# Dynamic filters: squares of two tile pairs summed on TensorE instead of GpSimd, and TensorE's sums placed between the next chunk's taps

## The reference

```python
h = x
for _ in range(5):
    t = gelu(einsum('oc,bchw->bohw', W1, h) + b1)
    k = einsum('oc,bchw->bohw', W2, t) + b2          # C * 9 channels
    k = k.reshape(B, C, 9, H, W)
    k = k / (norm(k, axis=2) + EPS)
    y = sum(patches(h) * k, axis=2)                  # 3x3 neighbourhood
    h = h + alpha * y
```

## Time and profile before

| | |
|---|---|
| median of 3 runs | 20082.18 us (20081.55 to 20100.58) |
| the profiled execution's own time | 20080.48 us |
| its span | 20078.7 us |
| layer of dynamic filters in it | about 15,565 to 20,079 us |
| TensorE matmul / VectorE / ScalarE / GpSimd busy over the whole span | 62% / 52% / 28% / 47% |
| mean granted TensorE clock over the whole span | 0.736 |

### The profile page before, as it was taken

The page is one execution under the profiler, slowest core; times in us unless marked ns, Lnnn a source line. Parts: engine busy times, 40 slices in busy tenths (PEclk is TensorE's granted clock), DMA queues, the critical chain, the costliest instruction groups (busy, mean ns, idle before and its releaser), DMA issues. The chain is left out here.

```text
span 20078.7 us, 217701 instructions
## 1 busy us (share of the span) xinstructions
PE 12353.6 (62%) x73490; PEld 6114.7 (30%) x73490; DVE 10535.6 (52%) x14652; ACT 5526.4 (28%) x7765; POOL 9453.1 (47%) x8026
## 2 busy tenths in 40 slices
PE   5553699999999202333333333333358899999998
PEld 2551366666666101111111111111112333333332
DVE  4557544444444333443443444344422788888887
ACT  1114333333333000000000000000010666666666
POOL 0113100000000106886887788688800787878787
PEclk9999856656666556666666666666679999999999
DMA  4104222222222494335334433533342112121201
GB/s 94 33 21 102 55 38 36 37 38 36 36 37 38 135 195 111 95 95 131 95 95 107 120 95 95 131 96 95 95 86 58 33 22 42 21 42 22 42 19 30
DMA packets 1399772, 1408.47 MB, mean 70 GB/s; under 512 B 771709, under 2 KB 1116045, under 8 KB 1383565
## 3 DMA queue, kind: packets, MB, share of 16 engines
q1 hardware_dynamic: 1106892, 742.84, 18.5%
q0 software_dynamic: 221184, 604.27, 10.4%
q10 hardware_dynamic: 70976, 50.83, 0.8%
HBM read 1036.74 MB, written 276.84 MB: 65 GB/s over the span
## 5 line engine op out<-in xcount | busy, mean ns | idle before, releaser
L1359 POOL DMA_INDIRECT dc_g<-corners,dc_idx x4608 | 5253.7, 1140 | 1326.0 <-issue 1260.9
L1954 POOL TENSOR_TENSOR df_sq<-df_sq 128x512 f32<-128x512 f32 x1920 | 2713.0, 1427 | 1866.6 <-ACT df_sq L1902 1839.5
L1432 PE MATMUL dc_ps<-ident,dc_s 128*128 128x128 f32 x2560 | 674.0, 428 | 4296.9 <-DVE dc_s L1523 4294.8
L1079 POOL TENSOR_TENSOR nz_vp<-nz_vp,nz_den 128x2048 f32<-128x2048 f32 x16 | 105.8, 6610 | 4814.7 <-DMA nz_den<-den_d 4814.7
L1515 DVE TENSOR_TENSOR dc_g<-dc_g,dc_wt 128x2304 f32<-128x2304 f32 x512 | 1308.6, 2556 | 2001.0 <-DMA dc_g<-corners,dc_idx 2000.9
L1902 ACT ACTIVATE df_sq<-df_pk,vecs 128x512 f32<-128x512 f32 x2880 | 1921.1, 685 | 1326.0 <-DVE df_pr L2056 1309.2
L2056 DVE SCALAR_TENSOR_TENSOR df_pr<-df_pk,vecs,df_h 128x512 f32<-128x512 f32 x2880 | 2047.6, 741 | 407.1 <-PE df_pk L1840 264.5
L1432 PEld LDWEIGHTS dc_ps<-ident,dc_s 128*128 128x128 f32 x2560 | 472.0, 218 | 4480.6 <-DVE dc_s L1523 3352.1
L1392 ACT ACTIVATE dc_st<-dc_ps 128x512 f32<-128x512 f32 x640 | 327.0, 607 | 4934.2 <-PE dc_ps L1432 4934.2
L1840 PE MATMUL df_pk<-df_t,df_wp 64*128 64x512 f32 x3840 | 1389.8, 642 | 364.7 <-ACT df_sq L1902 302.1
L916 DVE TENSOR_REDUCE at_mx<-at_pt 128x4 f32<-128x512 f32 x1024 | 707.8, 691 | 1605.4 <-PE at_pt L779 1605.4
(11 more groups left out here) (271 smaller groups left out, 19428.1 us busy)
## 6 DMA issues: line engine op xcount, KB each, us to landing
df_h<-df_h SPq DMA_DIRECT2D x160, 512.0 KB, 7.1
dc_g<-corners,dc_idx POOLq DMA_INDIRECT x4608, 2.8
corners<-dc_xt SPq DMA_DIRECT2D x16, 4160.0 KB, 41.5
dc_xp<-x SPq DMA_DIRECT2D x8, 4096.0 KB, 40.8
cv_xp<-x SPq DMA_DIRECT2D x8, 4096.0 KB, 50.0
y<-sp_p SPq DMA_DIRECT2D x128, 192.0 KB, 2.8
y<-sp_p SPq DMA_DIRECT2D x64, 384.0 KB, 4.3
at_a<-y SPq DMA_DIRECT2D x64, 384.0 KB
```

Source lines behind the costliest of these rows:

```text
L1359: nc.gpsimd.indirect_dma_start(gt[:, r, k, :, :].rearrange("p a c -> p (a c)"), None, image, bass.IndirectOffsetOnAxis(ap=idx[:, s, r, k:k ...
L1432: i = nc.tensor.transpose(ps[:, j, 128 * r:128 * r + 128], sm[:, r % 2, 128 * j:128 * j + 128], env.ident[:, :])
L1954: nc.gpsimd.tensor_tensor(a, a, sq[:, (KK * n + other) % RING, :], ALU.add).then_inc(nadded, 1)
```

## The change

GpSimd adds squares 2 into 0 and 3 into 1, as before, and no longer 4 into 0 and 5 into 1: four adds a chunk are left (`ADDS = 4`). TensorE sums the tiles 0 and 1 and the tiles 4 and 5 of the squares, four matmuls in place of two. `sums` is split into `products(n, i)` with i = 0 to 3 and `squares(n, i)` with i = 0 and 1, two matmuls each. They are set between the taps of the next chunk. The joins of VectorE are split: the squares of chunk n - 1 are joined behind product 7 and the products of chunk n - 2 behind product 1. The rings hold 18 tiles. ScalarE's `root`, `log` and `seed` stand one tap later, and so do VectorE's checks and most of its refinements.

```diff
-    BANKS, RING = 5, 15
+    BANKS, RING = 5, 18
+    ADDS = 4
...
-            def sums(n):
-                pe.wait_ge(product, KK * n + KK)
-                if n:
+            def products(n, i):
+                pe.wait_ge(product, KK * n + (2 * i + 2 if i < 3 else KK))
+                if i == 0 and n:
                     pe.wait_ge(yjoined, n)
...
+                for s in range(2):
+                    half = py[64 * s:64 * s + 64, :]
+                    if i < 3:
+                        last = nc.tensor.matmul(half, pair[:, :], pr[:, (KK * n + 2 * i + s) % RING, :], start=(i == 0), stop=False,
+                                                tile_position=(0, 64 * s))
+                    else:
+                        last = nc.tensor.matmul(half, env.ident[:, 64 * s:64 * s + 64], pr[:, (KK * n + 8) % RING, :],
+                                                start=False, stop=True, tile_position=(0, 64 * s))
                 last.then_inc(ysummed, 1)
...
+            def squares(n, i):
+                if i == 0:
+                    pe.wait_ge(nadded, ADDS * n + 2)
+                    if n:
+                        pe.wait_ge(njoined, n)
+                else:
+                    pe.wait_ge(squared, KK * n + 6)
+                for s in range(2):
+                    k = 4 * i + s
+                    last = nc.tensor.matmul(pn[64 * s:64 * s + 64, :], pair[:, :], sq[:, (KK * n + k) % RING, :],
+                                            start=(i == 0), stop=(i == 1), tile_position=(0, 64 * s))
+                if i == 1:
+                    last.then_inc(nsummed, 1)
...
             for n in range(NC):
-                for k in range(6):
-                    tap(n, k)
-                if n:
-                    sums(n - 1)
+                for i in range(3):
+                    tap(n, 2 * i)
+                    tap(n, 2 * i + 1)
+                    if n:
+                        products(n - 1, 0) if i == 2 else squares(n - 1, i)
                 if n + 1 < NC:
                     hid(n + 1)
                 for k in range(6, KK):
                     tap(n, k)
-            sums(NC - 1)
+                    if n:
+                        products(n - 1, k - 5)
...
# ScalarE
-                if k == 6 and n:
-                    act.wait_ge(nsummed, n)
...
-                    if q and (c, k) in ((0, 7), (0, 8)):
-                        root(q - 1, k - 7)
-                    if q and (c, k) in ((1, 0), (1, 1)):
-                        log(q - 1, k)
-                    if q and (c, k) in ((1, 2), (1, 3)):
-                        seed(q - 1, k - 2)
+                    if q and (c, k) in ((0, 8), (1, 0)):
+                        root(q - 1, c)
+                    if q and (c, k) in ((1, 1), (1, 2)):
+                        log(q - 1, k - 1)
+                    if q and (c, k) in ((1, 3), (1, 4)):
+                        seed(q - 1, k - 3)
...
# GpSimd
-                add(n, 0, 4, 1)
-                add(n, 1, 5, 2)
+                singles(n)
                 if q and c == 2:
                     scale(q - 1, 2)
-                singles(n)
                 add(n, 6, 7)
...
# VectorE
-            CHECK = {(1, 6): 0, (1, 8): 1, (2, 1): 2, (2, 3): 3}
-            REFINE = {(2, 5): 0, (2, 7): 1, (3, 1): 2, (3, 3): 3}
+            CHECK = {(1, 7): 0, (2, 0): 1, (2, 2): 2, (2, 4): 3}
+            REFINE = {(2, 6): 0, (2, 8): 1, (3, 2): 2, (3, 4): 3}
...
+                    if n >= 2 and k in (0, 2, 4, 8):
+                        dve.wait_ge(ysummed, 4 * (n - 2) + min(k // 2, 3) + 1)
+                    if n >= 2 and k == 6:
+                        dve.wait_ge(yjoined, n - 1)
...
-                    if k == 5 and n:
-                        join(n - 1)
+                    if k == 1 and n >= 2:
+                        join_products(n - 2)
+                    if k == 7 and n:
+                        join_squares(n - 1)
```

More of the change, by code:

```diff
@@ L1843, in tap @@
                     nc.tensor.matmul(pk[:, j % BANKS, :], ws[:, k - 6, :], t[:, n % 2, :], start=True, stop=True).then_inc(tapped, 1)
-            def sums(n):
-                pe.wait_ge(product, KK * n + KK)
-                if n:
+            def products(n, i):
+                pe.wait_ge(product, KK * n + (2 * i + 2 if i < 3 else KK))
+                if i == 0 and n:
                     pe.wait_ge(yjoined, n)
-                for k in range(6):
-                    s = k % 2
-                    nc.tensor.matmul(py[64 * s:64 * s + 64, :], pair[:, :], pr[:, (KK * n + k) % RING, :], start=(k < 2), stop=False,
-                                     tile_position=(0, 64 * s))
@@ L1853, in sums @@
                 for s in range(2):
-                    last = nc.tensor.matmul(py[64 * s:64 * s + 64, :], env.ident[:, 64 * s:64 * s + 64],
-                                            pr[:, (KK * n + 8) % RING, :], start=False, stop=True, tile_position=(0, 64 * s))
-                last.then_inc(ysummed, 1)
-                pe.wait_ge(nadded, 6 * n + 4)
-                if n:
-                    pe.wait_ge(njoined, n)
-                for s in range(2):
-                    last = nc.tensor.matmul(pn[64 * s:64 * s + 64, :], pair[:, :], sq[:, (KK * n + s) % RING, :], start=True, stop=True,
-                                            tile_position=(0, 64 * s))
@@ L1863, in sums @@
-                last.then_inc(nsummed, 1)
+                    half = py[64 * s:64 * s + 64, :]
[5 more added lines that the diff above has]
+                                                start=False, stop=True, tile_position=(0, 64 * s))
@@ L1875, in _ @@
                     tap(n, k)
-            sums(NC - 1)
+                    if n:
+                        products(n - 1, k - 5)
+            for i in range(2):
+                squares(NC - 1, i)
+            for i in range(4):
+                products(NC - 1, i)
         @block.scalar
@@ L1951, in add @@
                 if earlier:
-                    pool.wait_ge(nadded, 6 * n + earlier)
+                    pool.wait_ge(nadded, ADDS * n + earlier)
                 a = sq[:, (KK * n + into) % RING, :]
@@ L1980, in _ @@
                     scale(q - 1, 3)
-                add(n, 6, 8, 5)
+                add(n, 6, 8, 3)
                 if q and c == 1:
@@ L1992, in _, with join_products, join_squares @@
             dve.wait_ge(link, 3)
-            def join(n):
+            def join_products(n):
                 q, c = n // CH, n % CH
-                dve.wait_ge(ysummed, n + 1)
+                dve.wait_ge(ysummed, 4 * n + 4)
                 dve.wait_ge(sadded, n + 1)
                 nc.vector.tensor_tensor(yr[:, q % 2, c, :], py[:, :], pr[:, (KK * n + 6) % RING, :], ALU.add).then_inc(yjoined, 1)
+            def join_squares(n):
+                q, c = n // CH, n % CH
                 dve.wait_ge(nsummed, n + 1)
-                dve.wait_ge(nadded, 6 * n + 6)
+                dve.wait_ge(nadded, ADDS * n + ADDS)
                 nc.vector.tensor_tensor(nr[:, q % 2, c, :], pn[:, :], sq[:, (KK * n + 6) % RING, :], ALU.add).then_inc(njoined, 1)
@@ L2068, in _ @@
                         refine(q - 1, REFINE[c, k])
-            join(NC - 1)
+            join_products(NC - 2)
+            join_squares(NC - 1)
+            join_products(NC - 1)
             for i in range(CH):
```

## The result

The changed kernel takes 20266.86 us (median of 4, 20258.59 to 20272.56) against 20081.86 us before (median of 4). The ratio is 1.009, with a 95% interval from 1.0073 to 1.0108: 185 us slower. The profiled execution took 20262.01 us, its span is 20260.1 us.

The account below looks back on a forecast made before the run. TensorE was taken to bound three of four chunks, ScalarE c = 1. From 20082 us, three 13.15 us chunks less 1.11 in c = 1 add 79, clock falls 68: 20229, forecast 20230 us, 8-in-10 range 19985 to 20325.

Parts of the forecast that it names:

- the sign: Whole kernel: chances against the time before were slower 0.70, faster 0.17, the same 0.13.
- Changes of split: TensorE's order: 12 changes a chunk at 0.14 or 0.20 us, 2.0 us, making the chunk 13.15 us.
- The two kinds that had no row: Whole array to sums, sums to half-row taps: unseen before, together 0 to 1.02 us a chunk; upper end taken.
- Bank waits: TensorE's taps waiting for squares to free a bank: the new order leaves at least 5 us, so these waits go.
- Chunk c = 1: ScalarE's chunk: 16.28 us instead of 17.39, a gain of 1.11 us, with TensorE idle 3.1 us at its end.
- the moved square: ScalarE's stretch in c = 1: one of seven squares goes ahead of it, worth 0.57 us, leaving 15.58 us.
- The clock: TensorE after idling in c = 1: a fall costs up to 1.7 us; one in two groups assumed, +68 us.
- VectorE: Work unchanged, c = 2 about 13.3 us, level with TensorE; join done by about 5.6 us, products at 6: no wait, but closely.
- GpSimd, nothing on the path: GpSimd's dropped adds: 913 us of busy time go, but 0 on the path.
- The rivals: Three other outcomes for the whole kernel: faster (0.17), no change (0.13), slower still (0.08), against forecast 0.62.
- The faster one: Unseen changes of split on TensorE cost little: chunk 12.47 us, kernel 19998 us; with nothing 12.13 and 19919; chance 0.17.
- slower still: VectorE's join late in c = 0 and c = 2, product 8 late in c = 0: +160 us, 20390 us; chance 0.08.

Follow-up runs that it names:

- e3: Changed kernel's work in another TensorE order, five changes of split a chunk in place of 12, sums in longer blocks: 19904.04 us, ratio 0.9906.
- e6: Changed kernel with ScalarE's root, log and seed put back one tap earlier, where the kernel before has them: 20053.78 us, ratio 0.9985.
- e2: The order alone: changed kernel with all six adds on GpSimd and one pair of squares on TensorE: 20188.68 us, ratio 1.0048.
- e7: e3 with ScalarE's root, log and seed one tap earlier: 19951.98 us, ratio 0.9933.
- e4: Changed kernel plus three unused whole-array matmuls on TensorE at the end of each chunk c = 1: 20166.28 us, ratio 1.0037.
- e5: e3 with the old division of work, six adds on GpSimd and one pair of squares on TensorE: 19961.14 us, ratio 0.9937.

## Why the prediction was right, and where it was off

The time lies in the range, 37 us above the forecast of 20230 us, and the sign was given 0.70.

- **Changes of split.** Right, and shown: 1.01 to 1.06 us for each step that follows another kind. The two kinds that had no row came in at the upper bound. A chunk is 13.27 us, not 13.15: with 2.0 us for twelve changes I had rounded each down by about 0.01 us. Over three chunks and 80 groups that is 29 us too little. (In the rival's sum the low end of 12.13 us a chunk gives 19916 us, not 19919.) e3 shows the reverse: seven changes fewer, 1.2 us a chunk.
- **Bank waits.** Right: TensorE waits for no square in c = 2, 3 and 0, where all the time is busy.
- **Chunk c = 1.** Right in size, 16.28 us, and 2.95 us of idle time where 3.1 was worked out. The sum holds, but the sentence that counts the moved square as a gain of 0.57 us hides that the move itself costs 1.5 us (e6), since the stretch also starts 2.07 us later, the distance from tap 7 to tap 8.
- **The clock.** Right in kind, small in size: 1.6 us a fall, but in 52 of 64 groups instead of in half. That is 0.45 us a group more, 36 us.
- **VectorE.** This step was off, in the harmless direction. I had its work unchanged and c = 2 at about 13.3 us, level with TensorE; it is 10.37 us there, mostly since checks and refinements became shorter. And I had the first products 6 us after tap 0 and the join done by 5.6. My own prices put these products at 5.2 us (three pairs of taps, two of squares, each with a change of split), which with a join at 5.6 is a miss of 0.4 us. The trace has 5.19 and 4.59. That the meeting is met was right by luck.
- **GpSimd, nothing on the path.** This step was off for the same reason: I left out that its adds lengthen VectorE's operations. With six adds the join would come too late even for the changed kernel's place (e2, worked out and not run by itself). And in the groups with `residual`, where VectorE does come late in c = 0, the price fell. These are 14 and not 16, as the last two of the 16 do this work behind the last chunk. They take 59.5 us on average in the changed kernel, 2.1 over its others, where before they take 58.0, 3.3 over the usual 54.74. That is 1.2 us each, 16 us.
- **The rivals.** None came. The faster one needed cheap changes of split, and the "slower still" one came in e2 only, as its place and price were named.

Put together: 3 x 13.27 + 16.28 - 54.74 = 1.35 us a group, 108 us; falls of the clock 52/64 x 1.6 x 80 = 104 us; less 16 us in the groups with `residual`; less 18 us, because 19 groups of the kernel before take 55.6 or 55.7 us instead of 54.74. That is 178 us, where the two profiled executions are 181.5 us apart and the medians 185.

So that the time lies only 37 us above the forecast is in part luck: chunk and clock were 65 us short, and 34 us that were not in the sum go the other way.

It stays open why 12 of the 64 groups have no fall. They stand five groups apart wherever no `residual` lies between, but no run here was made for it. The rings of 18 tiles in place of 15 were not tried by themselves either.

## What to carry to other kernels

Count how often TensorE's order changes between matmuls that split the array differently: here each change costs 0.14 to 0.20 us, about a fifth of the 0.86 us that a step takes, and interleaving to hide a wait for banks paid twelve of them a chunk to save 1 to 2 us. The same interleaving in few, longer blocks (e3) keeps the cover and saves the time. Then look at where the idle time that remains comes to lie, since what runs behind it may run at half the clock.

## What the runs showed of the hardware beyond that

- In the changed kernel one idle time of 2.95 us was followed by 1.2 GHz in 52 of 65 groups, and one of 3.5 us, behind a chunk with `residual`, in 14 of 14. One of 1.39 us was so in none of the 61 usual groups of e6, but 0.4 and 2.0 us behind a `residual` in 12 of 14. Pieces of 1.14, 0.49 and 1.76 us had a fall in 16 of 64 groups (e3), but 0.85, 0.48 and 1.82 us in 32 of 64 (e7). What differs between e3 and e7 is not settled.
- GpSimd's adds lengthen VectorE's operations that read two SBUF tiles. Two updates of the changed kernel, the second beside adds of GpSimd:

```profile
18081.08 0.74 DVE L2036 SCALAR_TENSOR_TENSOR df_h<-df_y,df_alpha,df_h 128x512 f32<-128x512 f32 x1
...
18081.97 2.95 POOL L1967 TENSOR_TENSOR df_sq<-df_sq 128x512 f32<-128x512 f32 x2 [4.06 <-ACT df_sq L1915]
...
18082.40 1.38 DVE L2036 SCALAR_TENSOR_TENSOR df_h<-df_y,df_alpha,df_h 128x512 f32<-128x512 f32 x1
```

  Over the layer, the 128 updates with no GpSimd instruction beside them take 0.74 us on average and the 128 that overlap one 1.06; checks take 0.74 us without overlap and 1.71 when GpSimd is busy throughout. Products, which read PSUM, take 0.74 to 0.75 us either way. The number of adds alone doesn't set the mean: a refinement is 0.98 us in the changed kernel but 1.27 in e6, 1.28 in e3 and 1.33 in e4 with the same four adds, 1.35 before and 1.49 in e5 with six. The Trainium skill (SBUF — State Buffer, SBUF: two separate sides) says that the two engines lock a shared pair of ports against each other when VectorE has two SBUF inputs; these runs agree.
